# The beginning of a two-layer graph network kernel: sort and values interleaved, edge slots of 128

## The reference

```
xn = layernorm(x)
x = x + rgcn2(xn, edges, types) + mixer0(xn)      # layer 0
x = x + experts0(layernorm(x))
x = x + gat2(layernorm(x), edges) + mixer1(...)   # layer 1
x = x + experts1(layernorm(x))

rgcn: sums = segment_sum(x[src], dst * 8 + type); mean = sums / max(count, 1)
      out  = einsum('nri,rio->no', mean, W) + x @ root + b
mixer0: qkv = xn @ W_qkv + b; phi = relu(heads of q, k @ random_features.T)
      out  = phi_q @ (phi_k.T @ v) / 256 ... @ W_proj + b
```

## Time and profile before

| what | before |
|---|---|
| median of three executions | 2403.89 us (2403.42 to 2406.47) |
| the profiled execution, its own time | 2420.97 us |
| its span in the profile | 2419.2 us |
| PE / DVE / ACT / POOL busy | 88% / 59% / 39% / 19% |
| granted clock of TensorE, mean | 0.943 |
| first projection of mixer 0 on TensorE | starts at 89.19 us |
| relation products and slots | about 294 to 609 us |

### The profile page before, as it was taken

How to read it: one execution, slowest core, us unless ns; L and a number is a source line. 1 busy time by engine, 2 the same in 40 slices (tenths; PEclk the granted TensorE clock), 3 DMA queues, 4 the chain that set the end, 5 groups by cost and what they waited for, 6 DMA issues and landing times. The chain is left out here.

```text
span 2419.2 us, 32227 instructions
## 1 busy us (share of the span) xinstructions
PE 2134.1 (88%) x12845; PEld 2045.4 (85%) x12845; DVE 1429.5 (59%) x2288; ACT 951.5 (39%) x1252; POOL 450.8 (19%) x230
## 2 busy tenths in 40 slices
PE   4898999999899999999969849788888868999994
PEld 4787999999899999999849849687778857999994
DVE  8645445554565133333458864358884676888885
ACT  1234156665342021111127722125512224777772
POOL 4772300000300633444010022211120010000001
PEclk9899999999999999999969979898989987999997
DMA  3412223332432111110159951110122027999995
GB/s 103 138 31 75 74 96 111 128 118 89 144 114 72 59 59 40 40 59 20 46 175 334 313 201 59 46 44 27 45 70 79 14 100 275 356 366 367 365 365 186
DMA packets 158238, 326.92 MB, mean 135 GB/s; under 512 B 14120, under 2 KB 99336, under 8 KB 158090
## 3 DMA queue, kind: packets, MB, share of 16 engines
q1 hardware_dynamic: 133354, 265.68, 31.3%
q10 hardware_dynamic: 18976, 43.33, 5.1%
q0 software_dynamic: 5760, 15.86, 2.1%
HBM read 278.24 MB, written 46.51 MB: 134 GB/s over the span
## 5 line engine op out<-in xcount | busy, mean ns | idle before, releaser
L618 PE MATMUL banks<-weight_hi,xt_hi 128*128 128x384 f32 (+2 forms) x2208 | 743.1, 337 | 69.8 <-DVE xt_lo L1379 14.3
L621 PE MATMUL banks<-weight_lo,xt_hi 128*128 128x384 f32 (+2 forms) x2208 | 727.8, 330 | 0.0
L622 PE MATMUL banks<-weight_hi,xt_lo 128*128 128x384 f32 (+2 forms) x2208 | 727.5, 329 | 0.0
L618 PEld LDWEIGHTS banks<-weight_hi,xt_hi 128*128 128x128 f32 x2208 | 427.4, 194 | 82.0 <-issue 27.6
L621 PEld LDWEIGHTS banks<-weight_lo,xt_hi 128*128 128x128 f32 x2208 | 427.2, 193 | 0.4 <-issue 0.2
L622 PEld LDWEIGHTS banks<-weight_hi,xt_lo 128*128 128x128 f32 x2208 | 426.7, 193 | 0.0
L1829 DVE TENSOR_TENSOR weight_lo<-weight_raw,weight_hi 128x2304 fp32r<-128x2304 f32 (+2 forms) x153 | 339.7, 2241 | 65.2 <-ACT weight_hi L1115 65.2
L1115 ACT ACTIVATE weight_hi<-weight_raw 128x2304 fp32r<-128x2304 f32 (+2 forms) x153 | 287.7, 1885 | 128.7 <-DMA weight_raw<-L_ffn_w_in 74.0
L818 POOL TENSOR_TENSOR weight_hi<-weight_raw,columns 128x2304 fp32r<-128x2304 f32 (+1 forms) x23 | 95.7, 4160 | 784.0 <-PE banks L618 360.9
L2405 PE MATMUL banks<-held_hi,a_rel 128*128 128x384 f32 (+1 forms) x550 | 172.5, 342 | 9.7 <-DVE acc_rows L1626 5.6
L618 PE MATMUL banks<-weight_hi,hT_hi 128*128 128x384 f32 (+1 forms) x442 | 153.2, 347 | 21.5 <-DVE hT_lo L1839 14.3
(11 more groups left out here) (397 smaller groups left out, 3663.6 us busy)
## 6 DMA issues: line engine op xcount, KB each, us to landing
weight_raw<-L_ffn_w_in SPq DMA_DIRECT2D x102, 1152.0 KB, 7.5
weight_raw<-L_gnn_W_in SPq DMA_DIRECT2D x32, 1152.0 KB
weight_raw<-L_ffn_W_in SPq DMA_DIRECT2D x17, 1152.0 KB, 7.2
products<-bias_rows SPq DMA_DIRECT2D x80, 192.0 KB, 1.9
slot_in<-slot_rows ACTq DMA_DIRECT2D x34, 384.0 KB, 4.9
slot_out<-bias_rows ACTq DMA_DIRECT2D x34, 384.0 KB, 6.3
weight_raw<-L_ffn_W_in SPq DMA_DIRECT2D x17, 576.0 KB, 7.3
product_back<-products SPq DMA_DIRECT2D x10, 960.0 KB, 4.7
```

The costliest lines, as they stand in the source:

```text
L618: ins = pe.matmul(dst, s[0], m[0], start=start, stop=False)
L621: pe.matmul(dst, s[0], m[1], start=False, stop=False)
L622: return pe.matmul(dst, s[1], m[0], start=False, stop=stop)
```

## The change

It has four parts.

1. **Memory and order at the beginning.** The sort's buffers are moved from the values' memory to that of `phi_k`, `phi_qT` and later tiles, the first `end_phase` of the three engines is gone (the others are renumbered), and the values are evicted between the sort's steps. PSUM banks of the values are renumbered (`v_bank`) and waits follow them. The reduction over the slots' groups is done with slots on partitions (125 x 40) and transposed by TensorE.
2. **Who splits.** The two value units and the first mixer unit are split by ScalarE and VectorE (`unit_hi`, `unit_lo`), no longer by GpSimd.
3. **First DMAs.** SyncE issues the three edge loads ahead of the rows; ScalarE issues the random features, the two biases and `qk_bias` at once, ahead of its waits. TensorE transposes the random features ahead of the rows, and ScalarE and VectorE evict them ahead of the normalisation.
4. **Slots of 128.** 120 slots of 128 edges instead of 80 of 256, one or two beside each relation product; a slot is two matmuls. Even slots' one-hots come from VectorE, odd ones' from ScalarE. The first half that comes back is split beside the loop's last three products instead of behind them, the loads of halves 1 and 2 stand ahead of those of the root weights in SyncE's queue, and `part_back_lo` of later halves stands behind the first tile of `add_means` instead of ahead of it.

```diff
-SLOT = 2 * P
+SLOT = P
...
+        EARLY = 4
+        RF_BANK, SORT_BANK, GROUP_BANK = 7, 1, 4
...
+        def v_bank(j):
+            return (j + 2) % 8
...
+        def slots_beside(n):
+            return range(n * SLOTS // CHUNKS, (n + 1) * SLOTS // CHUNKS)
...
+            for k in range(STAGES):
+                sp.wait_ge(part_out[k], 16 * len(range(k, BACKS * TILES, STAGES)))
+            sp.wait_ge(part_full, CHUNKS)
+            for h in range(1, BACKS):
+                back_load(h)
             pair_load(U_ROOT2, "L0_gnn_root2")
...
-            for c in range(2):
-                split(Unit(U_V + c), UNIT)
-
             pool.wait_ge(filled, 16)
             pool.wait_ge(pos_ready, 1)
-            begun = 0
-            split(Unit(U_MIX), KD * P)
...
             for j in range(SET):
-                col, t = j // TILES, j % TILES
-                act.wait_ge(prod_used, PR_V0 + j + 1)
-                act.activation(value_cols(col, t, 0), by_head(v_f[j % 2]), ACT.Copy).then_inc(v_hi, 1)
+                value_hi(j)
+                if j == TILES + 1:
+                    unit_hi(U_MIX)
...
                 for n in range(2):
-                    for half in range(2):
-                        ins = pe.matmul(ps[:, 2 * (s % 2) + n, 0:HALF], src_hot[k][:, half, :], dst_hot[k][:, half, cols_half(n)],
-                                        start=(half == 0), stop=(half == 1))
+                    ins = pe.matmul(ps[:, 2 * (s % 2) + n, 0:HALF], src_hot[k][:, :], dst_hot[k][:, cols_half(n)], start=True, stop=True)
...
             for n in range(CHUNKS):
                 part_rows(0, n, False)
-                edge_slot(n, n % TILES == FULL)
+                for s in slots_beside(n):
+                    edge_slot(s, n % TILES == FULL and s == slots_beside(n)[0])
...
                 for c in range(2):
-                    if layer == 0 and 2 * r + c + 1 < HALVES:
-                        part_back_lo(2 * r + c + 1)
                     for t in range(TILES):
+                        if layer == 0 and t == 1 and 2 * r + c + 1 < HALVES:
+                            part_back_lo(2 * r + c + 1)
```

More of the change, by code:

```diff
@@ L761, in _ @@
                 sp.wait_ge(part_out[k], 16 * (CHUNKS // STAGES))
[L762 to L765, removed]
+            for h in range(BACKS, HALVES):
+                sp.wait_ge(agg_full, TILES * (h - BACKS + 1))
                 back_load(h)
@@ L1438, in _, with value, value_lo, values @@
             vec.tensor_copy(in_row[:, :], rank[:, :, EDGE_COLS - 1]).then_inc(sort_row, 1)
+            unit_lo(U_V + 1)
+            def value(j):
+                vec.wait_ge(prod_full, PR_V0 + j + 1)
+                if j >= 2:
+                    vec.wait_ge(v_lo, j - 1)
+                vec.tensor_tensor(v_f[j % 2][:, :], ps[:, v_bank(j), 0:WCOL], bias_row[0][:, wcols(j // TILES)], ALU.add).then_inc(prod_used, 1)
+            def value_lo(j):
+                vec.wait_ge(v_hi, j + 1)
+                hi, lo = [value_cols(j // TILES, j % TILES, h) for h in range(2)]
+                vec.tensor_tensor(lo, by_head(v_f[j % 2]), f32(hi), ALU.subtract).then_inc(v_lo, 1)
+            def values(first, last):
+                for j in range(first, last):
+                    value(j)
+                    if j > first:
+                        value_lo(j - 1)
+                value_lo(last - 1)
+            vec.wait_ge(bias_in, 32)
+            values(0, 3)
             vec.wait_ge(sort_sum, 2)
-            order.step(vec.tensor_scalar(need_i[:, :], ps[0:EDGE_ROWS, SORT_BANK + 1, 0:GROUPS], float(SLOT - 1), None, ALU.add))
+            order.step(vec.tensor_scalar(need_i[:, :], ps[0:EDGE_ROWS, SORT_BANK, GROUPS:2 * GROUPS], float(SLOT - 1), None, ALU.add))
             order.wait()
@@ L1527, in keys_values @@
                 vec.tensor_tensor(kv_own(kv[1]), part, kv_own(f32(kv[0][:, :])), ALU.subtract).then_inc(B_done, 1)
[L1529 to L1536 removed]
+            projection(0, 0)
+            order.wait()
+            order.step(vec.tensor_copy(spot_i[:, :], pos_f[:, :]))
+            order.wait()
+            order.step(vec.tensor_scalar(low_i[:, :], spot_i[:, :], P - 1, None, ALU.bitwise_and))
+            order.step(vec.tensor_scalar(sub_i[:, :], spot_i[:, :], 7, None, ALU.arith_shift_right))
+            order.wait()
+            vec.scalar_tensor_tensor(pos_i[:, :], low_i[:, :], float(SLOTS), sub_i[:, :], ALU.mult, ALU.add).then_inc(pos_ready, 1)
             unit_lo(U_MIX + 1)
[L1538 removed]
+            vec.wait_ge(filled, 16)
+            for part in kv:
+                order.step(vec.memset(f32(part[:, :]), 0.0))
             for j in range(PAIRS):
```

321 lines of the change are left out of this document (157 added, 164 removed).

## The result

The changed kernel takes 2380.73 us (median of 4 runs, 2379.98 to 2383.25), the kernel before 2404.39 in runs beside it: ratio 0.9893, 95% interval 0.9866 to 0.992, so about 24 us less. Forecast were 2362 and a range from 2353 to 2376. The sign was right; the gain is little more than half of the 41.5 us that the sum gave.

What follows compares the result with a forecast made beforehand. TensorE was taken to bound the relation products and slots, with waits ahead of 89 us and around 609 us. Terms 20.5 + 11.0 + 10.0 = 41.5 us took 2420.97 to 2379.5, median 2362, range 2353 to 2376.

Steps and rivals of the forecast that it cites:

- The start: Beginning of the kernel: statistics start at 16.6 us (12 to 20.5), `kT_lo` at 73.0, head pairs 22.6 us earlier.
- I take 15: First DMAs: `qk_bias` lands at 15 us, at most 19, and sets the start of the statistics.
- The scatter takes some back: Projection's weight unit behind the scatter: lands at 206.5, wanted at 204.4; 2.1 us lost, 20.5 us remain.
- my shift of 17.1 us to the median: Whole program: profiled execution forecast at 2379.5; the median lies 17.1 below it, so 2362.
- the scatter bounds more: Rival at the scatter: `pos_i` comes at 80 instead of 74.8, the front gives 15.3, time 2368; chance 0.14.
- The slots: Slot loop: 320 to 240 slot matmuls at 0.1375 us each save 11.0 us; bounds 8 and 11.
- Nearly 2 us of slack stay: Slot loop: VectorE's additions keep nearly 2 us of slack even when two slots stand together.
- the slower rival: Slot loop becomes bound by VectorE's additions, TensorE waits at 40 products with two slots; 2422 us, chance 0.04.
- The end of the loop: After the last slots: first wait shrinks from 4.10 to about 2.3, second of 5.64 goes; 10.0 us, bounds 3 and 12.
- Sum: Whole kernel: beginning 20.5, slots 11.0 and end of the loop 10.0 give 41.5 us.

Runs made afterwards that it cites:

- rf_alone: The changed kernel with the turning of the random features no longer waiting for the load of the query and key biases; 2374.27 us.
- proj_first: The changed kernel with SyncE's two loads of the projection's weight halves ahead of its wait for the scatter; 2363.88 us.
- front_only: The changed kernel with slots of 256 edges and the old end of the loop, so the new beginning alone; 2401.68 us.
- before_proj_first: The kernel before, with SyncE's two loads of the projection's weight halves ahead of its wait for the scatter; 2405.06 us.
- after_again: The changed kernel, unchanged, run and profiled again; 2384.78 us.
- back_undone: The changed kernel with the end of the slot loop as in the kernel before; 2393.06 us.
- lo_in_quarters: The changed kernel with VectorE's low part of a weight half made in four pieces, one after each of four products; 2375.03 us.
- all_three: The changed kernel with projection loads ahead of the scatter wait, random features not waiting for biases, and low parts in four pieces; 2353.43 us.
- before_again: The kernel before, unchanged, run for a second profile; 2405.18 us.

## Why the prediction was wrong

**The start.** "I take 15" for the landing of `qk_bias`: it was 20.2, above the upper bound of 19. The statistics came 5.2 us late. Part of this was won back behind them: `kT_lo` 1.9 late. That the passes were slow by GpSimd's splits, and are fast without them, was right. The Trainium skill's rule ("SBUF — State Buffer", Who interferes with whom), by which VectorE and GpSimd lock each other out of a port pair, fits: each slow pass lasts as long as one of GpSimd's split instructions, 4.38 or 5.40 us beside 4.3 and 5.2, and the mean of 4045 ns in the earlier trace rows is that of four such passes and a first one of 0.68, which began before GpSimd did; without splits a pass takes 676 ns. Its other rule ("DMA: Bandwidth & Descriptors", Issuing engines are not separate DMA queues), that the queues of SyncE and ScalarE share the same 16 engines, fits in its direction. I had priced it at 2 us: in rf_alone the rows of x are there at 16.11, against 9.31 before, 6.8 us later, of which I had given 1.3 to the three edge issues. Which of the loads beside them takes the rest wasn't tried.

**The scatter takes some back.** This is the step that failed. I had 2.1 us: the unit lands at 206.5 and is wanted at 204.4. It landed at 210.2 and was wanted at 194.6 (where proj_first splits it): 2.1 + 3.7 + 9.8 = 15.6. The 3.7 are the load's issue at 204.37 instead of 201.6, since the scatter starts 2.6 us later, and its landing 5.8 instead of 4.9 us after. The 9.8 come from the date that I subtracted from: 226.99 in the earlier trace rows belonged to an execution in which this point was 13.4 us later than in the second one; 3.6 go the other way, 3.3 of them since `kT_lo` moved by 19.3 (94.2 to 74.9) and not by 22.6. The beginning was thus worth 3.2 us (277.9 to 274.7), not 20.5, and front_only gives 2.9. Neither is sharp: against before_proj_first, whose first sum comes at 273.3, the beginning gives nothing, and the interval of front_only holds 1. The first sum of one beginning also moves with the clock: in the six profiles with the changed beginning as it stands it comes at 275.2 to 276.7 in the three that have the second spell at the lower level (after_again, back_undone, front_only), and at 273.4 to 274.7 in the other three.

The excess of that execution wasn't spread over the program, as my shift of 17.1 us to the median took for granted: 13.4 of it lay inside the stretch that the change moves, where it hid the wait. The step that failed is thus the date at which ScalarE wants the unit, 204.4 by the forecast and 194.6 in fact, and with it the wait: 2.1 us forecast, 14.5 measured at ScalarE and 15.5 at TensorE. My rival "the scatter bounds more" named the mechanism and put it down to a late `pos_i` (76.3, little late); its own price, 15.3 for the front, was far off too.

**The slots.** 240 matmuls and the periods of 3.45 and 3.73 are there. "Nearly 2 us of slack stay": yes against the mean load, but a weight half of 2.56 us stands in that stream, which the text said only under the slower rival. In 11 periods it costs 0.3 to 0.6 us, 5.3 in all by lo_in_quarters, so the term measures 4.9 instead of 11.0, below its bound of 8.

**The end of the loop.** 10.0 forecast, 9.5 to 10.0 measured; the first wait 2.75 (2.3), the second gone, the clock at 1.00 there.

**Sum.** 3.2 + 4.9 + 10.0 = 18.1, and 0.6 between the first root sum and the first slot: 18.7 to the last mean (749.7 to 731.0). Stages that the change doesn't touch add to it or take from it: from the first to the last `att_p` it is 278.6 to 278.8 us in the three profiles with the old beginning, 275.6 to 276.2 in eight of the eleven with the new one, and 277.3, 278.6 and 279.2 in the others (all_three, all_three_slots256, front_only). It goes with the granted clock: in the six long ones TensorE is at its lower level for 51.2 us of this stretch, in the eight short ones for 37.6 to 47.8 (traces, worked out). What sends the clock down there more often wasn't tried. With its 2.8 the change comes to 21.5; the medians say 22 to 24. More than that the traces don't tell of what lies behind the last mean: it takes 1653 to 1656 us in the three profiles of kernels with the old beginning, and 1642 to 1660 in the others. So the forecast of 2379.5 for the profiled execution, beside the measured 2380.06, was met by luck: 13.6 us of a long execution and 8.6 behind the last mean (before_again against after) stand in for what the terms lack.

## What to carry over

- A date of the trace from which a saving is subtracted, to see what becomes late next, is to be taken from an execution whose time is near the median. If the profiled one is long, find where the excess lies before the sum is shifted by it: it may be the cover of a wait.
- When work is moved ahead of a long transfer, list what stands behind that transfer in the same issuing queue, and who wants it when. Two loads that didn't depend on the scatter cost all but 3 of 19 us here.
- Slack counts against the longest single piece of work in the stream, not against the mean load. Cutting that piece cost nothing that shows here: four pieces of 0.75 us stand for one of 2.56.

## What was not expected of the hardware

- One and the same program lost 7.9 us of TensorE's time between 118 and 214 us in one execution and none in another, in stalls of 0.3 to 2.2 us, some put down to "issue" and some to another engine, with the clock at 0.98 and 1.00. What caused them isn't known.
- Whether VectorE or GpSimd goes first is not settled by the code. VectorE's five passes that write `xn_rows` take 19.9 and 20.0 us in the two profiles of before and 15.2 in before_proj_first, whose code is the same up to there. In before the second pass starts at 15.73, behind GpSimd's first split (15.43), and takes 4.38; in before_proj_first it starts at 15.55, ahead of that split (15.88), and takes 0.67. In before_again the two start within 0.02 us of each other, and the pass is slow. This is the 4.6 us by which `kT_lo` is early there. The one-line summaries, before and then before_proj_first (shortest, median, longest ns):

```profile
L1359 DVE TENSOR_SCALAR xn_rows<-x_rows,norms x5: 679/4382/5395, 15.1 to 29.6; 128x768 f32<-128x768 f32 x5
```

```profile
L1359 DVE TENSOR_SCALAR xn_rows<-x_rows,norms x5: 672/4380/5397, 15.0 to 25.8; 128x768 f32<-128x768 f32 x5
```

- A DMA of 6 KB in 1536 pieces of 4 bytes landed 17.4 us after its issue beside the loads of the start (10.6 in the earlier trace rows), and the issue behind it, of the list of -1, held ScalarE for 7.93 us; before, where that issue stood ahead of `qk_bias`, it took 0.34. No run tried which of its neighbours holds it. The changed kernel's DMA issues and ScalarE's timeline:

```profile
qk_bias<-L_mix_b_qkv_in ACTq DMA_DIRECT2D x1, 6.0 KB, 17.4
```

```profile
3.30 7.93 ACTq L978 DMA_DIRECT2D edges_sorted<-fill_i  x1
```

- Of two loads of 1152 KB issued together behind the scatter (204.37 and 204.85), the first was in use 5.8 us after its issue; the one issued alone in the earlier trace rows had landed after 4.9 us.
